# A second hand-written order for all engines of a two-layer attention kernel, with fixed PSUM banks

## The reference, cut to what matters

```python
query = side + b_self                      # [256, 256]
key   = concat([x + b_prev, side + b_self]); value = concat([x, side])
q, k, v = query @ Wq + bq, key @ Wk + bk, value @ Wv + bv       # 16 heads of 16
score_prev = q k_prev^T * SCALE, masked to the first seq_len keys of x
score_self = sum(q * k_self) * SCALE       # one extra key for each row: itself
w = softmax(concat([score_prev, score_self]))
x1 = x + (w_prev @ v_prev + w_self * v_self) @ Wo + bo
s = tanh(x1 @ W1 + b1) @ v                 # second layer: one score per row
out = x1 + softmax(masked s) @ x1 / count  # mask by kind: prefix, postfix or all but itself
```

## Time and profile before

| | us |
|---|---|
| three runs | 303.89, 306.69 (median), 310.06 |
| the profiled execution | 307.28 |
| its span, first to last instruction | 305.5 |
| busy PE / DVE / ACT / POOL | 238.5 / 178.4 / 152.5 / 64.8 |
| mean granted clock of TensorE | 0.932 of full |
| a full period (batch n+1 prepared, batch n-2 finished) | 30.6 |

### The profile page before, as it was taken

The page is one execution under the profiler, slowest core; times in us unless marked ns, Lnnn a source line. Parts: engine busy times, 40 slices in busy tenths (PEclk is TensorE's granted clock), DMA queues, the critical chain, the costliest instruction groups (busy, mean ns, idle before and its releaser), DMA issues.

```text
span 305.5 us, 5479 instructions
## 1 busy us (share of the span) xinstructions
PE 238.5 (78%) x1988; PEld 180.8 (59%) x1988; DVE 178.4 (58%) x367; ACT 152.5 (50%) x281; POOL 64.8 (21%) x80
## 2 busy tenths in 40 slices
PE   2667487798888988898889888888898788586433
PEld 1657366566665767576757675766576546264323
DVE  3763547656766577657765776576658486214431
ACT  4133114566655656565656565656565274553220
POOL 9400100030151034103410341034104111411400
PEclk9978779799999999999999999999999797779957
DMA  6459615834952854285426542833274110200100
GB/s 164 139 195 208 185 68 146 171 106 163 199 165 101 185 134 141 100 194 128 139 98 176 149 141 92 190 71 124 101 189 79 36 39 2 72 0 0 36 1 34
DMA packets 28283, 35.57 MB, mean 116 GB/s; under 512 B 4440, under 2 KB 24672, under 8 KB 28256
## 3 DMA queue, kind: packets, MB, share of 16 engines
q1 hardware_dynamic: 27616, 33.12, 40.9%
q0 software_dynamic: 640, 2.10, 2.0%
HBM read 20.26 MB, written 14.69 MB: 114 GB/s over the span
## 4 chain that ended last, share of the span: by engine, by line
PE 56%; DVE 15%; issue 11%; ACT 9%; DMA 5%; SPq 2%; POOL 1%; ACTq 0%; DVEq 0%; POOLq 0%
PE ps_any L1013 14%; PE ps_any L1056 9%; PE ps_max L1094 7%; PE ps_any L1120 5%; PE ps_any L1019 5%; PE ps_any L1190 3%; PE ps_exp L1108 3%; PE ps_any L1136 3%; DMA q_rows<-mt_sb 2%; PE ps_any L1167 2%; ACT pool_p L620 2%; DVE s_max L828 2%; DVE prod L814 2%; PE ps_any L1175 2%; ACT q_full L523 2%
## 5 line engine op out<-in xcount | busy, mean ns | idle before, releaser
L828 DVE TENSOR_REDUCE s_max<-ps_max 128x4 f32<-128x1024 f32 x64 | 78.0, 1219 | 37.5 <-PE ps_max L1094 37.4
L542 ACT ACTIVATE pt<-ps_exp 128x1024 f32<-128x1024 f32 x64 | 65.5, 1024 | 52.3 <-PE ps_exp L1108 51.8
L1094 PE MATMUL ps_max<-k_rows,q_rows 49*128 49x256 f32 x256 | 33.1, 338 | 10.0 <-DVE s_max L828 7.5
L1120 PE MATMUL ps_any<-pt,v_aug 128*32 128x256 f32 x512 | 36.3, 403 | 0.3 <-ACT pt L542 0.3
L437 POOL TENSOR_TENSOR attn<-num,rden 128x256 f32<-128x256 f32 x16 | 9.6, 623 | 113.7 <-DVE rden L871 113.7
L1108 PE MATMUL ps_exp<-q_rows,k_rows 51*128 51x256 f32 x256 | 27.9, 296 | 6.4 <-DMA q_rows<-mt_sb 5.8
L1094 PEld LDWEIGHTS ps_max<-k_rows,q_rows 49*128 49x128 f32 x256 | 19.8, 190 | 22.0 <-DVE s_max L828 10.3
L1108 PEld LDWEIGHTS ps_exp<-q_rows,k_rows 51*128 51x128 f32 x256 | 20.4, 192 | 8.8 <-DMA q_rows<-mt_sb 7.1
L423 POOL TENSOR_TENSOR q_lo<-q_full,q_hi 128x512 fp32r<-128x512 f32 x7 | 8.9, 1274 | 74.9 <-ACT q_hi L528 74.9
L1013 PE MATMUL ps_any<-w_hi,in_hi 128*128 128x256 f32 x64 | 21.2, 331 | 3.0 <-DVE w_lo L710 2.6
L1120 PEld LDWEIGHTS ps_any<-pt,v_aug 128*32 128x32 f32 x512 | 13.8, 112 | 11.1 <-issue 2.1
(11 more groups left out here) (136 smaller groups left out, 535.8 us busy)
## 6 DMA issues: line engine op xcount, KB each, us to landing
q_rows<-q_spill SPq DMA_DIRECT2D x32, 192.0 KB, 4.3
k_rows<-k_spill SPq DMA_DIRECT2D x32, 192.0 KB
q_spill<-q_hi SPq DMA_DIRECT2D x16, 256.0 KB, 2.5
k_spill<-k_hi SPq DMA_DIRECT2D x16, 256.0 KB, 2.5
s_sb<-in_fside_BxSxS SPq DMA_DIRECT2D x8, 256.0 KB, 6.2
x_sb<-in_x SPq DMA_DIRECT2D x8, 256.0 KB, 5.9
q_spill<-q_lo SPq DMA_DIRECT2D x8, 256.0 KB, 2.7
k_spill<-k_lo SPq DMA_DIRECT2D x8, 256.0 KB, 2.1
```

The costliest lines, as they stand in the source:

```text
L542: nc.scalar.activation(pt[:, 2 * j % 8:2 * j % 8 + 2], ps_exp[:], ACT.Exp).then_inc(p_ready, 1)
L828: nc.vector.tensor_reduce(s_max[:, j // MJ, :, j % MJ, :], ps_max[:], AX.X, ALU.max).then_inc(max_found, 1)
L1094: last = pe.matmul(ps_max[:, e, t], q_rows[b % 2][rows, j, P * t:P * t + P], k_rows[b % 2][rows, j, :], start=True, stop=True)
L1120: last = pe.matmul(bank[32 * c:32 * c + 32, 0, :], v_aug[b % 2][:, t, h, :], pt[:, h % 8, t, :], start=(t == 0), stop=(t == KB - 1), skip_ ...
```

## The change

The steps and their instructions are the same; the order on every engine, the period in which some steps stand, and the bank of each use are new.

On PE, TS, TX, Q and the first half of the keys (K0) of a batch move one period earlier (they are now for batch n+2), and K1 stands in the next period, third from its start. AT moves from period n's batch n-2 to the end of the period before (batch n-1), so that WO stands fifth in a period. VS, V, PO and NAT are in halves that may stand apart. Score steps are no longer in pairs but spread singly.

On DVE `result`, `products` and `keys_lo` follow the first maximum; `denominators` stands after maximum 5 and `attention_lo` last. On ACT the order is: exps 2, k_hi, exps 3, pv copy 0, exps 4, x1t_hi, exps 5, pv copy 1, self exps, exps 6, tanh, exps 7, maximum rows 0, v_self, pv copies 2 and 3, x1_hi, s_self, side_hi, pool exps, exps 0, pool_hi, x_hi, v_aug, queries, exps 1, at_hi, maximum rows 1. Each `ps_any` use has a fixed bank, the third number in `USES`.

```diff
-    ("PV0", -1, "pv_copied", 4, 1),
-    ("MT1", -1, "mt_copied", 2, 2),
...
+    ("K1", 1, 3, "k_lo", 2, 2),
+    ("WO", -2, 0, "x1_done", 1, 1),
+    ("PV0", -1, 2, "pv_copied", 4, 1),
+    ("VS", 1, 0, "vs_copied", 1, 1),
+    ("X1T", -2, 3, "x1t_lo", 1, 1),
...
+    ("PO", -2, 2, "out_done", 1, 1),
+    ("MT1", 0, 3, "mt_copied", 2, 2),
 ]
+FIRST_USES = [("TS", 0), ("TX", 0), ("Q", 0), ("K0", 0), ("K1", 0), ("VS", 0), ("SS", 0), ("V", 0),
+              ("TS", 1), ("TX", 1), ("Q", 1)]
 def shared_banks():
-    free, last, found = [None] * BANKS, -1, {}
-    for period in range(-1, NB + 3):
-        for step, offset, reader, per, done in USES:
-            if not 0 <= period + offset < NB:
-                continue
-            last = (last + 1) % BANKS
-            found[step, period + offset] = (last, free[last], len(found))
-            free[last] = (reader, (period + offset) * per + done)
+    row = {use[0]: use[2:] for use in USES}
+    order = FIRST_USES + [(step, period + offset) for period in range(-1, NB + 4) for step, offset, *_ in USES]
+    free, found = [None] * BANKS, {}
+    for step, b in order:
+        if not 0 <= b < NB or (step, b) in found:
+            continue
+        bank, reader, per, done = row[step]
+        found[step, b] = (bank, free[bank], len(found))
+        free[bank] = (reader, b * per + done)
     return found
...
             place_q(0, 1)
             place_k(0, 1)
-            for n in range(B + 1):
-                if live(n + 2):
+            for n in range(B + 2):
+                if 2 <= n + 2 < B:
                     load(n + 2)
-                if live(n - 1):
-                    place_max(n - 1, 1)
-                if live(n + 1):
-                    spill_q(n + 1)
-                    spill_k(n + 1)
-                if live(n):
-                    place_max(n, 0)
-                if live(n + 1):
-                    place_q(n + 1, 0)
-                    place_k(n + 1, 0)
-                    place_q(n + 1, 1)
-                    place_k(n + 1, 1)
-                if live(n - 1):
-                    load_residual(n - 1)
+                if live(n - 2):
+                    load_residual(n - 2)
+                    place_max(n - 2, 1)
+                if 1 <= n - 1 < B:
+                    place_k(n - 1, 1)
+                if 1 <= n < B:
+                    spill_q(n)
+                    spill_k(n)
+                if live(n - 1):
+                    place_max(n - 1, 0)
+                if 1 <= n < B:
+                    place_q(n, 0)
+                    place_q(n, 1)
+                    place_k(n, 0)
         @block.gpsimd
...
-                if live(n - 2):
-                    attention(n - 2)
-                    residual(n - 2)
-                if n == 0:
-                    queries_lo(1)
-                elif live(n + 1):
+                if 1 <= n + 1 < B:
                     queries_lo(n + 1)
+                if live(n - 1):
+                    self_values(n - 1)
+                if live(n - 2):
+                    x1_low(n - 2)
                 if live(n - 3):
                     store(n - 3)
                 if live(n - 1):
-                    self_values(n - 1)
-                if live(n - 2):
-                    x1_low(n - 2)
+                    attention(n - 1)
+                    residual(n - 1)
             pool.wait_ge(out_stored, 16 * B)
...
                 last.then_inc(bv_product_ready, 1)
             def period(n):
...
+                if live(n):
+                    score_for_max(n, 0)
+                if live(n - 1):
+                    score_for_exp(n - 1, 2)
+                if 1 <= n + 1 < B:
+                    keys(n + 1, 1)
+                if n + 1 == 1:
                     bv_product()
...
+                if live(n - 2):
+                    output_product(n - 2)
+                if live(n - 1):
+                    score_for_exp(n - 1, 3)
+                    pv(n - 1, 0)
+                if live(n):
+                    score_for_max(n, 1)
+                if live(n - 1):
+                    score_for_exp(n - 1, 4)
+                if 1 <= n + 1 < B:
+                    self_values(n + 1, 0)
+                if live(n - 2):
+                    x1_transposed(n - 2)
+                if live(n - 1):
+                    score_for_exp(n - 1, 5)
+                if live(n):
+                    score_for_max(n, 2)
+                if live(n - 1):
+                    pv(n - 1, 1)
+                    score_for_exp(n - 1, 6)
+                if live(n):
+                    score_for_max(n, 3)
+                if 1 <= n + 1 < B:
+                    self_values(n + 1, 1)
+                if live(n - 2):
+                    pool_hidden(n - 2)
+                if live(n - 1):
+                    score_for_exp(n - 1, 7)
+                if live(n):
+                    score_for_max(n, 4)
+                if live(n - 1):
+                    pv(n - 1, 2)
+                if live(n):
+                    max_to_rows(n, 0)
+                if live(n - 1):
+                    pv(n - 1, 3)
+                if live(n):
+                    score_for_max(n, 5)
+                if live(n - 2):
+                    pool_scores(n - 2)
+                if 1 <= n + 1 < B:
+                    self_scores(n + 1)
+                if 2 <= n + 2 < B:
+                    side_transposed(n + 2)
+                if live(n - 1):
+                    naturals(n - 1, 0)
+                if 1 <= n + 1 < B:
+                    values(n + 1, 0)
+                if live(n - 1):
+                    naturals(n - 1, 1)
+                if 1 <= n + 1 < B:
+                    values(n + 1, 1)
+                if live(n):
+                    score_for_exp(n, 0)
+                    score_for_max(n, 6)
+                if live(n - 2):
+                    pool_transposed(n - 2)
+                if 2 <= n + 2 < B:
+                    x_transposed(n + 2)
+                    queries(n + 2)
+                if live(n):
+                    score_for_max(n, 7)
+                    score_for_exp(n, 1)
+                if live(n - 1):
+                    attention_transposed(n - 1)
+                if 1 <= n + 2 < B:
+                    keys(n + 2, 0)
+                if live(n - 2):
+                    pooled(n - 2, 0)
+                    pooled(n - 2, 1)
+                if live(n):
+                    max_to_rows(n, 1)
             pe.wait_ge(ident_ready, 1)
             side_transposed(0)
...
             biases()
             keys(0, 0)
             keys(0, 1)
-            self_values(0)
+            self_values(0, 0)
+            self_values(0, 1)
             self_scores(0)
-            values(0, (0, 1))
+            values(0, 0)
+            values(0, 1)
             side_transposed(1)
             x_transposed(1)
             queries(1)
-            for n in range(B + 3):
+            for n in range(-1, B + 2):
                 period(n)
```

More of the change, by code:

```diff
@@ new lines @@
+    ("Z", -2, 2, "tanh_done", 1, 1),
+    ("PV2", -1, 3, "pv_copied", 4, 3),
+    ("MT0", 0, 1, "mt_copied", 2, 1),
+    ("PV3", -1, 2, "pv_copied", 4, 4),
+    ("SB", -2, 1, "masked_done", 2, 2),
+    ("SS", 1, 0, "ss_copied", 1, 1),
+    ("TS", 2, 3, "st_lo", 1, 1),
+    ("NAT0", -1, 2, "num_done", 2, 1),
+    ("V", 1, 0, "v_copied", 1, 1),
+    ("NAT1", -1, 1, "num_done", 2, 2),
+    ("PT", -2, 3, "pt_lo", 1, 1),
+    ("TX", 2, 1, "xt_lo", 1, 1),
+    ("Q", 2, 2, "q_full_done", 1, 1),
+    ("AT", -1, 0, "at_lo", 1, 1),
@@ L629, in period @@
             def period(n):
-                nxt, now, prv, old = n + 1, n, n - 1, n - 2
-                if live(prv):
-                    exps(prv, 2)
-                    pv_copy(prv, 0)
-                    max_rows_copy(prv, 1)
-                if live(nxt) and n > 0:
-                    side_hi(nxt)
-                    x_hi(nxt)
-                if live(prv):
-                    self_exps(prv)
-                    exps(prv, 3)
-                if live(nxt) and n > 0:
-                    queries(nxt)
@@ new lines, in period @@
+                if live(n - 3):
+                    result(n - 3)
+                if 1 <= n + 1 < B:
+                    products(n + 1)
+                if live(n - 1):
+                    self_args(n - 1)
+                if 1 <= n + 1 < B:
+                    keys_lo(n + 1)
+                if n + 1 == 1:
+                    weight_lo(3)
+                if n + 1 == 1:
+                    output_bias()
+                if live(n - 2):
+                    add_residual(n - 2)
+                    hide(n - 2)
```

306 lines of the change are left out of this document (119 added, 187 removed).

## The result

Four runs took 275.44, 277.45, 278.87 and 279.23 us (median 278.16), against 303.89 to 310.06 before (median 306.64 of four): ratio 0.9085, 95% interval 0.8981 to 0.9189. In a later series the same kernel took 272.78 to 279.33 us (median 276.32 of six, ratio 0.9039, 0.8975 to 0.9103). The forecast was 275 in 267 to 289. The profiled execution is the fastest of the four, 275.44 us with a span of 273.7; the forecast of the span was 274.0.

A forecast was written before the change was run, and what follows sets the result against it. PE was taken as the bound: 26.78 us busy plus 3.8 of waits per full period. Savings 14.4 + 6.7 + 0.1 + 1.4 + 2.5 + 6.4 = 31.5 off the 305.5 span gave 274.0, forecast 275 us, range 267 to 289.

The forecast's parts named there:

- The full periods: Periods 2 to 5: from 30.6 to 27.0 us each, busy row 26.78 plus 0.2 of waits; 14.4 us less.
- The end below (26.4): Full periods: 26.4 us, the layout as it stands, as the low end of a full period's length.
- The time to period 0 and period 0: Start: K0 of batch 1 adds 1.5 us before period 0; period 0 falls from 23.58 to 22.0; 0.1 less.
- Period 1: Period 1: from 24.70 to 23.3 us, 1.4 less.
- period 6: Period 6: without TS, TX, Q and K0, plus 1.0 for uncovered chains, 23.9 us; 6.7 less.
- Period 7: Period 7: from 25.71, the chain of maxima and rows 22.4 plus 0.8 for the lower clock; 2.5 us less.
- Period 8 up to AT: Period 8 to AT of batch 7: from 24.45 to 18.0 us, NAT(7) no longer behind PT(6); 6.4 less.
- rival A: Exp scores 4, periods 1 to 6: maxima's rows land late, each about 1.1 us longer, 282 us; chance 0.2.
- AT to the end: From AT of batch 7 to the end: same chain in both kernels, 22.4 us, 0 gained.
- B, DVE the bound: Full periods: DVE work ahead of maxima 1 and 6 costs 1.5 us each, 7.5 in all, 283; chance 0.14.
- C, no gain: Full periods: one late bank reader holds PE as long as the six old waits, 305 to 307 us; chance 0.05.
- D, the clock: Full periods: new waits drop PE to the lower clock, 12 us a period, 347 us, slower; chance 0.03.

The follow-up runs named there:

- e8: Changed kernel with four of the six matmuls of the second half of VS left out: 275.88 us, ratio 0.8934.
- e2: Changed kernel with K0 for batch n+1 moved back directly ahead of K1, in the bank table too: 286.17 us, ratio 0.9434.
- e3: Changed kernel with AT back inside the period, between K1 and exp scores 3, and WO behind `pv` 0: 286.16 us, ratio 0.9443.
- e6: Changed kernel with other banks for three start uses, and K0(1), max scores 1, maxima 1 and 2 moved in period 0: 272.77 us, ratio 0.8805.
- e9: Changed kernel with small unread matmuls filling PE's idle time before and in period 0 and in the last period: 275.63 us, ratio 0.893.
- e11: Changed kernel with small unread matmuls filling PE's idle time before and in period 0 only: 273.0 us, ratio 0.8885.
- e7: Changed kernel with four small unread DMAs issued ahead of the second group of maximum rows: 279.41 us, ratio 0.9208.
- e13: Changed kernel with three bank-table entries altered (WO to 3, AT to 2, PO to 0), order kept: 296.26 us, ratio 0.9709.
- e5: Changed kernel with other banks for three uses in the start (SS, V, TX): 275.14 us, ratio 0.8906.

## Why the prediction was right, and where it was not

- **The full periods**, the step that carries the forecast, were right in kind and failed in size: forecast 27.0, measured 26.13 to 26.15, 4 x 0.86 = 3.4 us further down over periods 2 to 5. The layout of the new order gave 26.2, which was right; the step that failed is "the busy row says 26.78. I take the busy row". A period without gaps is as long as its starts are apart, and recorded lengths overlap. The 0.2 of new waits do not appear either. The end below (26.4) was no lower bound. The reading behind it holds: all six waits are gone, PE is now the bound (e8), and K0 at the border is cover for the maxima (e2). AT's place is worth 0.52 a full period too (e3), but no wait shows why.
- **The time to period 0 and period 0** failed: forecast 32.9 and 22.0, measured 36.0 and 24.8, 5.9 us more in sum. K0(1) was counted, at 1.5. Left out were the waits of the fixed banks in a start without other work between them (0.69 + 0.29), and the clock: the bias matmuls took 3.4 instead of 2.0 us and K(0) 4.8 instead of 4.2, so that VS started 1.85 later (23.85 against 22.00) ahead of any wait for a bank, and period 0 ran at 0.79 against 0.86 before. On DVE, products, k_lo, w_lo and bias_out lie between maxima 0 and 1, from 37.70 to 40.84, and PE waits 4.1 us for maxima. e6 and e9 to e11 show that order and clock both count.
- **Period 1** 23.0 (23.3) and **period 6** 24.5 (23.9): within 0.7.
- **Period 7** 22.0 (23.2), 1.2 better: I had put in 0.8 for the lower clock, and the granted clock was 1.00 where the earlier trace rows had 0.87. The other 0.4 is not explained.
- **Period 8 up to AT** 16.3 (18.0), 1.7 better: clock again (0.4), and a landing counted twice. I added 1.3 of issue and 2.99 of landing, but in the earlier trace rows the landing begins at 261.43, and the issues of these rows began at 260.77: 264.42 - 260.77 = 3.65 from the first issue, not 4.3. The same sum set the margin of rival A. In the changed kernel the issue begins at 235.35 and exp scores 4 start at 238.72, held by an exponential and not by the rows, so 3.37 at most. The two make about 1.1 of the 1.7.
- **AT to the end** 22.5 (22.4), as said.
- **In sum** errors of -3.4, -0.3, -1.2 and -1.7 stand against +5.9 and +0.7. The span met its number to 0.3 us by cancelling: from the start of period 0 on, 36.4 us went (274.1 to 237.7) where I said 33.0, and the start before it cost 4.6 where I said 1.5. This is luck. The profile that meets the number is also the fastest of its four runs, which spread over 3.8 us; their median, 278.2, lies 3 us above the forecast of 275, that of the later series, 276.3, lies 1.3 above.

**The rivals.** A, rows late: refuted in full periods by e7 (1.35 us more, no wait); the margin was more than 1.3, not 0.5. B, DVE the bound: refuted by e8. C, no gain: it did not come, but e13 shows how near it lies, since late readers of two banks, above all of one, give back 18 of 28 us (296.26 - 278.16 of 306.64 - 278.16). D, the clock: it did not come; no idle piece of a full period was left, and every one stands at 1.00. Its mechanism is real (e13), at a smaller price than mine, 1.45 a period and not 12, because the clock rises again within the period. The trace of before held 1.00 in every full period, with six idle pieces of at most 1.0 us; in e13, with one of 2.04, a fall follows in three of four. The Trainium skill, TensorE: Matmul & The Clock Gate, "A second HAM failure mode: psum-queue depth-cycling", ties such swings to short idle times between groups while banks are cycled. The full periods do not agree: both kernels cycle four banks and stay at 1.00, the kernel before with six short idle times in each. Of these runs only e13 swings there, and it has a long one.

**Open:** of the 4.5 us that a full period gained, e2 and e3 give back 1.04 and 0.52; the moves behind the other 2.9 (Z and K1's bank, PT, PO, TX) were not undone one by one, and for them the evidence is that their waits are gone. What fixed banks alone are worth against banks taken in turn with this order was not tried. Why the start's clock varies between runs of one program is not known either.

## What to carry to other kernels

When an order leaves the bound engine no idle time, sum the distances between starts of its instructions, not their recorded lengths. Work moved across a period's border can pay as cover for a serial chain there (K0, e2), and it can pay more in the last batch, where the chain stands bare (AT, e3). The price is in the start, which deserves an order and banks of its own. Read a bank table with all users of a bank before changing an entry, and price a long wait of PE with the clock it can cost behind it.

## What the hardware showed unexpectedly

- In e13, after a wait of 2.04 us of PE in an otherwise full period, the granted clock is 0.50 from 121.5 to 124, at 1.45 us; this follows in three of four full periods, and in the fourth, after the same wait, the clock stays at 1.00. In e2 it is 0.50 from 65 to 66, behind the wait of 2.85, and stays at 1.00 behind the one of 2.28. Six waits of 0.2 to 1.0 a period never brought a fall in the full periods of the kernel before. So the length of one wait alone does not decide it; what does is open.
- In the start, K(0)'s matmuls step 0.43 apart and later 0.23, at a granted clock given as 1.00 for both. In e11 the same steps of 0.43 stand in a stretch given as 0.53. Where the two disagree, I take the steps as the sign of the level. In e11 PE had been kept busy there with dummies, and the clock fell all the same.
- Keeping PE busy is not shown to narrow the spread of the runs: e9 ranges over 1.3 us (275.19 to 276.5), but e5, without a dummy and in the same series, over 0.9 (274.57 to 275.42), and e11 over 5.0.
